# One patch step moved ahead of the attention scores in the filling slots of a ViT tower kernel on Trainium2

## What is computed

```python
patches = img.reshape(B, 3, 14, 14, 14, 14).transpose(0, 2, 4, 1, 3, 5).reshape(B, 196, 588)
h = concat([token, patches @ W.T + b]) + pos                 # (64, 197, 128)
# attention 1: state is decayed by 0.9 and increased by 0.1 k v^T for each token; out = (q . state) @ Wo + bo
h = h + attn(layernorm(h))
# router: logits = relu(x.mean(1) @ r_w1 + r_b1) @ r_w2 + r_b2, sel = argmax(softmax(logits))
# attention 2: softmax(q k^T / 4) v @ wo, 8 heads, with the weight set sel (8, 4 or 1 key heads)
h = h + gqa(layernorm(h), weights[sel])
```

## Time and profile before

| what | value |
|---|---|
| median of 3 runs | 818.92 us (818.77 to 820.72) |
| the profiled execution's own time | 817.79 us |
| its span, first to last instruction | 816.1 us |
| busy: TensorE, ScalarE, VectorE, GpSimd | 772.3, 602.4, 579.3, 399.1 us |
| mean granted TensorE clock in the span | 0.986 of full speed |
| TensorE busy in the first 12 to 66 us | 39.33 of 54 us, granted clock 0.91 |

### The profile page before, as it was taken

The page is one execution under the profiler, slowest core; times in us unless marked ns, Lnnn a source line. Parts: engine busy times, 40 slices in busy tenths (PEclk is TensorE's granted clock), DMA queues, the critical chain, the costliest instruction groups (busy, mean ns, idle before and its releaser), DMA issues.

```text
span 816.1 us, 25687 instructions
## 1 busy us (share of the span) xinstructions
PE 772.3 (95%) x8496; PEld 651.1 (80%) x8496; DVE 579.3 (71%) x1842; ACT 602.4 (74%) x1364; POOL 399.1 (49%) x954
## 2 busy tenths in 40 slices
PE   3687899999999999999999999999999999988996
PEld 2576688888888888888888888888888888876774
DVE  3246777778777777777778777877777777777771
ACT  3466478877888778777877888788878887656664
POOL 1467555555546555544555555554645555442000
PEclk9899999999999999999999999999999999999998
DMA  6556555555555555555455545555555555322320
GB/s 141 150 149 171 174 165 167 143 158 171 166 146 151 168 172 147 153 167 173 140 158 172 168 137 160 173 162 148 155 174 166 148 151 160 114 92 92 121 72 16
DMA packets 138704, 120.53 MB, mean 148 GB/s; under 512 B 12606, under 2 KB 138446, under 8 KB 138574
## 3 DMA queue, kind: packets, MB, share of 16 engines
q1 hardware_dynamic: 136898, 118.34, 49.5%
q10 hardware_dynamic: 1676, 0.57, 0.4%
HBM read 30.99 MB, written 6.46 MB: 46 GB/s over the span
## 4 chain that ended last, share of the span: by engine, by line
PE 86%; DVE 3%; SPq 2%; ACT 2%; issue 2%; DMA 2%; POOL 1%; ACTq 1%; POOLq 1%; DVEq 0%
PE ps L433 12%; PE ps L629 11%; PE ps L578 9%; PE ps L606 8%; PE ps L611 6%; PE ps L549 4%; PE ps L658 4%; PE ps L563 4%; PE ps L507 3%; PE ps L640 3%; PE ps L499 3%; PE ps L478 3%; PE ps L550 2%; PE ps L519 2%; PE ps L594 2%; PE ps L473 2%
## 5 line engine op out<-in xcount | busy, mean ns | idle before, releaser
L855 DVE TENSOR_REDUCE top<-ps 99x2 f32<-99x394 f32 x512 | 265.3, 559 | 103.2 <-PE ps L578 102.8
L996 ACT ACTIVATE prob<-ps 99x396 f32<-99x396 f32 x512 | 234.0, 497 | 72.6 <-PE ps L611 71.9
L934 ACT ACTIVATE packed<-img 84x686 f32<-84x686 f32 x128 | 178.2, 1400 | 0.9 <-DMA img<-in_x 0.9
L433 PE MATMUL ps<-cols,w_tok 126*128 126x196 f32 x640 | 123.4, 338 | 8.6 <-DMA cols<-packed 7.6
L606 PE MATMUL ps<-top_rows,pick_rows 64*99 64x198 f32 x1024 | 120.6, 267 | 2.1 <-ACT prob L996 1.4
L433 PEld LDWEIGHTS ps<-cols,w_tok 126*128 126x128 f32 x640 | 111.6, 195 | 10.2 <-DMA cols<-packed 8.6
L611 PE MATMUL ps<-stack 64*99 64x198 f32 x1024 | 113.6, 253 | 0.0
L606 PEld LDWEIGHTS ps<-top_rows,pick_rows 64*99 64x99 f32 x1024 | 85.1, 162 | 28.8 <-issue 22.2
L578 PE MATMUL ps<-stack 64*99 64x198 f32 x1024 | 103.6, 280 | 2.5 <-DVE top L855 2.4
L629 PE MATMUL ps<-prob,v_ones 99*32 99x198 f32 (+1 forms) x2048 | 101.6, 334 | 0.3 <-ACT prob L996 0.2
L367 POOL TENSOR_SCALAR xhat<-h,mv,rstd 99x128 f32<-99x128 f32 x114 | 89.7, 795 | 5.9
(11 more groups left out here) (148 smaller groups left out, 1555.9 us busy)
## 6 DMA issues: line engine op xcount, KB each, us to landing
stack<-qk SPq DMA_DIRECT2D x256, 198.0 KB, 2.5
img<-in_x SPq DMA_DIRECT2D x192, 150.1 KB
cols<-packed SPq DMA_DIRECT2D x128, 160.8 KB
cols<-packed SPq DMA_DIRECT2D x64, 128.6 KB
out<-h SPq DMA_DIRECT2D x64, 49.5 KB
out<-h SPq DMA_DIRECT2D x64, 49.0 KB
w_rows<-in_L_tok_W SPq DMA_DIRECT2D x1, 294.0 KB, 3.2
sets<-in_L_ffn_wo SPq DMA_DIRECT2D x3, 64.0 KB
```

Of the source, the lines that this page charges most:

```text
L433: last = nc.tensor.matmul(ps[:, CY, 0:N * N], w_tok[0:KROWS, s, :], cols[b.ring % 2][:, :, s, :], start=(s == 0), stop=(s == STEPS - 1))
L855: nc.vector.tensor_reduce(top[:, c // 4, first:first + 2], columns, AX.X, ALU.max, negate=True).then_inc(m_read, 1)
L934: last = nc.scalar.activation(packed[b.ring % 2][:, first:end, :], img[b.ring % IMGS][:, :].rearrange("p (x w) -> p w x", w=P)[:, first:en ...
L996: nc.scalar.activation(prob[:, c, :], ps[0:T, E0 + c % 2, 0:CHUNK], ACT.Exp, scale=DK ** -0.5).then_inc(exp_done, 1)
```

## The change

In the list `filling`, the three early patch steps of the arriving image stood behind the scores as one piece. Now step 0 stands ahead of the scores and steps 1 and 2 behind them:

```diff
                     (turn_normed1, turned), (turn_patches, patched), (project_z, turned), (route_hidden, routing),
-                    (scores, turned), (patches, arriving, 0, HEAD), (route_logits, routing),
+                    (patches, arriving, 0, 1), (scores, turned), (patches, arriving, 1, HEAD), (route_logits, routing),
                     (project_qk, projected), (weigh, turned), (turn_normed2, added),
```

## The result

| | before | changed |
|---|---|---|
| median, 14 runs each | 819.83 us (817.14 to 823.92) | 823.44 us (821.11 to 826.60) |
| changed / before | | 1.0042, 95% interval 1.0030 to 1.0055 |
| profiled execution, own time | 817.79 us | 826.60 us |
| span; mean granted clock | 816.1 us; 0.986 | 824.9 us; 0.981 |
| project_z in slots 6, 8, 10 | 44.29, 55.88, 68.64 | 46.66, 60.49, 76.63 |

By the ratio the change makes the kernel 3.4 us slower (0.42% of 819.8); the two medians lie 3.6 us apart. 1.75 us of the distance was there before the first changed slot: TensorE's first 10 patch passes after the setup start at 26.05 and not 24.30, since small setup loads landed 1.8 us later.

A forecast was written before the change was run, and what follows sets the result against it. TensorE bounds the middle and a two-slot chain of gather waits the fill; 1.8 us for the order plus 2.35 for the clock made 4.15, giving 823.1 us against the three-run median 818.92, range 820.3 to 825.3.

The forecast's parts named there:

- steps 1 and 2: Fill, slots 4 to 9: gathers land after the scores would be done, so scores follow the landing; landing to weighing 1.10 becomes 1.68.
- steps 2 and 3: Landing to weighing in a waiting slot: scores cost TensorE 0.58 us; mask path ties at 1.68; upper end 0.75.
- Slot 4's delay is gone: Slot 4's scores finish up to 0.6 later, but slot 5 waits 1.98 us for a gather behind SyncE's weight loads.
- slot 6 has room: Slot 6's gather is held by SyncE's queue; its 0.58 goes into the other loop, which has room.
- step 4: Which fill slots count: 5, 7 and 9, at 0.58 + 0.58 + 0.64 = 1.8 us; bounds nothing and 2.7.
- step 5: Longer waits in slots 7 and 9 bring half clock: 1.35 and 1.0, together 2.35 us; 1.67 at most per stretch.
- the chain alone: Rival: scores cost time in three slots, but new waits bring no half clock; 818.92 + 1.8 = 820.7 us; chance 0.20.
- the rival of one new stretch: Only one of slots 7 and 9 gets a half-clock stretch: 1.8 + 1.2 = 3.0 us, 821.9; chance 0.23.
- the forecast's two: Half-clock stretches in both slots 7 and 9: 1.8 + 2.35 = 4.15 us, 823.1; chance 0.42.
- the gap would be filled: Rival: step 0 runs while z is awaited, -1.1 to -2.2 us; chance 0.04, shared with a former half-clock stretch going missing.
- The signs to look for: Profile after: project_z of slots 6, 8, 10 late by 0.6, 1.2, 1.8 before the clock; first max_scores at 81.3 to 84.
- In parallel: From the first max_scores matmul on, both traces run alike, so the shift at 80 us is found at the end.

The follow-up runs named there:

- warm pair: Extra fp32 matmuls with unused results in the waits of slots 3 to 9, in before's order and the changed order: 818.93 and 820.56 us.
- even swaps: The kernel before with the changed order in slots 4, 6 and 8 only: 822.75 us, ratio 1.0030 to before.
- second profile: Both kernels run and profiled again with nothing changed: before 816.79 us, changed kernel 822.20 us.
- all three steps ahead: The kernel before with all three early patch steps, not just one, ahead of the scores: 823.66 us, ratio 1.0055 to before.

## Why the prediction was right, and where not

The total was right: 3.4 us slower (0.42%) where 4.15 was forecast, 823.44 us where 823.1 was. The working was right in its mechanism and wrong in one step and in its sizes, which partly cancelled. That the absolute times agree to 0.3 us is in part luck: the forecast started from the median of three runs, 818.92, and that of 14 runs is 819.83.

- **The wait moves ahead of the scores and puts them on the chain** (steps 1 and 2): shown by the chain after, and by the warm pair.
- **0.58 per waiting slot, 0.75 at most** (steps 2 and 3): 0.67 measured. Landing to weighing was met to 0.01 (1.67 for 1.68); the rest came between the weighing and the second turn, 0.64 us for 0.53. In slot 9 0.64 was forecast and 0.95 measured: 0.59 up to the weighing, and 0.37 behind it, where TensorE waits 0.85 us and not 0.49 for the second normalisation, which VectorE does behind the mask and the router's steps. All three together: 1.8 forecast, 0.67 + 0.67 + 0.95 = 2.3 by the rows, 1.2 to 2.4 by the runs of the warm pair.
- **"Slot 4's delay is gone" and "slot 6 has room"** (step 4): this failed. It read the one trace of before, in which slot 5's gather was held by SyncE and the odd slots waited. In the two profiles of the changed kernel slot 4 waits 1.88 and 2.40 us in one piece. Where the half clock then fell on slot 4, slots 4, 6 and 8 carried the loop, and slot 5 waited for nothing (even swaps) or 0.97 us (second profile). The even swaps alone cost 0.30%. That about three slots pay in an execution all the same is why the sum held, and the prediction had not reasoned that; it is luck.
- **The clock** (step 5): the size per stretch was near, 5.90 - 4.37 = 1.53 us in slot 7 for at most 1.67. In slot 9 of the first profile, 8.18 - 5.82 = 2.36 for 0.6 to 1.3, since the stretch lasted over 6 us. But not each long wait brings one, as 3.03 us in the second profile shows, and before has its own stretches in other places, with 10.2 us at half in the fill of both its profiles. In the runs the clock is left with 1.0 to 2.2 us of the loss, where the forecast had 2.35; by the plain kernels' own clocks it is 1.2.
- **The rivals**: the chain alone (0.20) is refuted as the whole by both profiles, in which new waits did bring half clock, though it may hold the larger share. By size the loss lies between the rival of one new stretch (3.0) and the forecast's two (4.15). That the gap would be filled did happen in slot 8 of the first profile, and bought nothing.
- **The signs to look for**: project_z of slots 6, 8 and 10 was late by 0.6, 2.9 and 6.2 us once the setup's 1.75 is taken off, for 0.6, 1.2 and 1.8 before the clock's part. The first max_scores matmul came at 87.48, outside the 81.3 to 84 that I gave, and outside also at 85.7 without the setup's 1.75; the second profile has 85.89. From there to the end of the span it is 737.4 us against 736.6, and 734.6 against 734.5 in the second profiles. "In parallel" holds only to about 0.8 us, since half-clock stretches also lie in this part: the first profile of the changed kernel has two between 90 and 114 us and that of before one, and each of them has one between 752 and 766 that both second profiles lack. The prediction took the clock as 1.00 from 90 to 700 from a mean in which the stretch at 90.7 can't be seen.

## What to carry to other kernels

Before an instruction is moved ahead to fill a gap, ask which wait it carries: in an in-order queue all that now stands behind it inherits that wait, and a gap of 0.4 us is worth nothing if it lies in front of a wait that ends last. Where two loops interlock, one trace tells which of them binds in that execution only; cost the edit in both. Here the gain lay in taking loads off the queue that issues the gathers, not in the order of the matmuls.

## What the hardware showed beyond what I expected

- The half-clock stretches of the fill lasted 3.4, 6.8 or 10.2 us, and lay elsewhere in each execution of the same code: from 22.5 and 39.6 us in one profile of before, from 24.1 and 37.8 in the other. Waits of 1.11, 1.70, 1.87, 2.40 and 2.55 us in the changed kernel came with one, waits of 1.88 and 3.03 us in it did not, nor did those of 1.93 and 1.88 us in slots 6 and 8 of the kernel with all three steps ahead. The length of a wait alone doesn't tell; the granted clock has to be read, and in more than one profile.
- Runs of one kernel on one core scattered by 817.1 to 823.9 us. Two causes are seen in the traces: how many half-clock stretches there are and where they lie (in 35 runs of before one with a mean granted clock lower by 0.001 is 0.4 us longer, by a straight line), and the landing of the small setup loads (VectorE's first sum of the position rows starts at 13.10 in one profile and at 14.93 in another). The loss of 3.4 us is half of that scatter, and only the many runs tell it from none.
